# Projection and V moved to the end of TensorE's quarter, and the transposes of h made in tiles of 64 only

## The chip, the cores and the metric

The kernel runs on one core of one Trainium2 chip. Its engines are TensorE (PE; its weight loads are shown apart as PEld), VectorE (DVE), ScalarE (ACT), GpSimd (POOL) and SyncE (SP), which here issues all transfers. The metric is the device time of one execution in microseconds, the median of several runs.

## The reference, cut to what matters

A macaron block on x of shape 16 x 512 x 128, in float32: half a feed-forward part, attention with its residual, half a feed-forward part again.

```python
x = x + 0.5 * ffn(layernorm(x), w_gate, w_up, w_down)
x = x + attn(layernorm(x), w_q, w_k, w_v, w_proj, b_proj, ln_gamma, ln_beta)
x = x + 0.5 * ffn(layernorm(x), w_gate, w_up, w_down)

def ffn(x, w_gate, w_up, w_down):          # hidden size 352
    h = silu(fp4_linear(x, w_gate)) * fp4_linear(x, w_up)
    return fp4_linear(h, w_down)
def fp4_linear(x, w):                      # blocks of 16 along the contraction
    return fp4_quant_dequant(x) @ fp4_quant_dequant(w).T
def attn(x, ...):                          # 16 heads of 64, 512 x 512 scores each
    o = softmax(q @ k.T * 64 ** -0.5) @ v
    y = o @ w_proj + b_proj + x
    return layernorm(y) * ln_gamma + ln_beta
```

## The kernel before

There are 16 images. In each, attention goes over 8 pairs of heads p, and each pair over 4 quarters s, one for each key tile of 128. `i = 8 b + p` counts the pairs over all images, and t = 4 p + s the 32 quarters of an image. Each engine has its own program, which runs over the same quarters with a body written out by hand; `steps` unrolls two images ahead and the last ones, and loops over two images at a time between them. Engines meet only at semaphores, each engine works strictly in its own order, and so a place in the body is the schedule. (The profile shows a 32-bit float matmul as two records, "x4" for a pair; a pair is two halves of 64 output partitions that run side by side.)

PE's quarter begins with `scores` (L943: eight matmuls into pS for ACT's exponential). At s = 3 the broadcast of the reciprocals follows (L1049, into pM). Then come `for_maxima` (L955, into pX, one or two pairs ahead, for the row maxima that DVE takes at L779), `times_v` (L970, into pO), and one piece that depends on s:

- s = 0: Q of pair i + 2 (L927, into pM), read by ACT (QH, L738) and then by DVE (QL, L901).
- s = 1: the projection of pair i - 3 (`project`, L991, into pX), added up by DVE in Yacc (L898); then K of pair i + 2 (L927, into pM), read by ACT (KH, L741) and then by DVE (KL, L905).
- s = 2: the row sums (L980, into pM).
- s = 3: a quarter of V (L1085, into pM), read by ACT (VA, L750).

The feed-forward parts of the neighbouring images run in between: F is the first one and works for the image after, L the last one and works for an image before. `first_ffn` and `last_ffn` give them pieces at fixed t, behind everything else of PE's quarter. On PE, F has the transposes of x at t = 0 (L239), gates at 1 to 4 (L256), ups at 5 to 8 (L267), the transposes of h at 12 to 15 (`pe_h`, L284), the down projection at 16 (`pe_down`, L295) and a transpose at 20. L has ups at 0 to 2 and 31, `pe_h` at 6 to 9, `pe_down` at 10, the transposes of x at 26 and gates at 27 to 30. Each part has one PSUM tile, pF, which its pieces use in turn.

h has 352 columns, two chunks of 128 and one of 96. `pe_h` transposes each chunk in two column tiles, 64 wide but for the last one of the third chunk, which is 32 wide. ACT copies all three into hqT, `pe_down` contracts them with wdT, the transposed w_down, and takes 96 rows of the third chunk. wdT is made at the start from a tile that POOL fills with zeros before the weights are loaded into it.

What the projection waits for: ON of pair i - 3 (`s_norm`), all row maxima of pair i + 1 (`s_max`, DVE L779 of the same quarter, since both use pX), and the Yacc add before it (`s_yacc`). `for_maxima` at s = 2 waits for the Yacc add of this projection. V waits for KL, for VA before it, and for ON (`s_norm`, DVE L888 of the same quarter), all for pM. K waits for QL, the row sums for KL, and the next Q for VA.

DVE's quarter: the reciprocal (s = 0), the feed-forward steps that read PSUM (silu L331, h L337), ON (s = 3), the maxima, the Yacc add (s = 1), QL (s = 0) or KL (s = 1), and then the other feed-forward steps (block maxima L165, rounding L186 and L188, moments of the norms). ACT's: the feed-forward reads of PSUM (tanh L310, copies L305 and L315), the exponential L731, the copies of this quarter, and the other feed-forward steps (L181, L142). POOL adds up exponentials for the row sums (L640, L646) and does the scalings of the quantization (L175, L193).

Of the kernel before, what the change touches and what calls it, by code (L numbers as in the profile page):

```python
# [13 lines left out]
ALU = mybir.AluOpType  # L14
# [6 lines left out]
NP = B * PAIRS  # L21
FF = 352
# [4 lines left out]
FP = 384  # L27
FT = FP // 128
# [36 lines left out]
def there(n, count):  # L65

    return not isinstance(n, int) or 0 <= n < count


def wait(eng, sem, count):  # L70

    if not isinstance(count, int) or count > 0:
        eng.wait_ge(sem, count)


def half(n):

    return slice(64 * n, 64 * n + 64)
# [118 lines left out]
class Ffn:  # L197
# [73 lines left out]
    def pe_h(self, pe, c, k):  # L271

        if k % 2 == 0:
            pe.wait_ge(self.qh.s_quant, 2 * c + k // 2 + self.w0 + 1)
        if k == 0:
            pe.wait_ge(self.s_h, 4 * c + 4)
        else:
            pe.wait_ge(self.s_hT, 4 * c + k)
        row = self.row(k)
        for ch in range(FT):  # L280
            for n in range(2):
                f0 = ch * 128 + 64 * n
                w = min(64, FF - f0)
                ins = self.nc.tensor.matmul(self.pF[64 * n:64 * n + w, ch * 128:(ch + 1) * 128], row[:, f0:f0 + w],  # L284
                                            self.ident[:, :], start=True, stop=True)
        ins.then_inc(self.s_hT_ps, 1)

    def pe_down(self, pe, c):

        pe.wait_ge(self.s_hT, 4 * c + 4)  # L290
        for t in range(T):
            for ch in range(FT):
                rows = min(128, FF - ch * 128)
                for n in range(2):
                    ins = self.nc.tensor.matmul(self.pF[half(n), t * D:(t + 1) * D],  # L295
                                                self.hqT[0:rows, ch, t * 128 + 64 * n:t * 128 + 64 * n + 64],
                                                self.wdT[0:rows, ch, :], start=ch == 0, stop=ch == FT - 1)
        ins.then_inc(self.s_down, 1)


# [75 lines left out]
def make_program(nc, x_in, w_q, w_k, w_v, w_proj, b_proj, gamma_in, beta_in, w_gate, w_up, w_down, out):  # L376
# [35 lines left out]
    with ExitStack() as scope:  # L412
# [95 lines left out]
        with nc.Block() as block:  # L508
            @block.sync
            def _(sp):  # L510
# [3 lines left out]
                for k, w in enumerate((w_gate, w_up)):  # L514
                    sp.dma_start(wraw[:, k, 0:256].rearrange("p (t d) -> p t d", t=2),
                                 w[0:256, :].rearrange("(t p) d -> p t d", p=128)).then_inc(s_wraw, 16)
                    sp.dma_start(wraw[0:FF - 256, k, 256:384], w[256:FF, :]).then_inc(s_wraw, 16)
                sp.dma_start(wraw[:, 2, 0:FF], w_down).then_inc(s_wraw, 16)
                for k, w in enumerate((w_q, w_k, w_v)):
                    sp.dma_start(w_raw[:, k, :], w).then_inc(s_raw, 16)  # L520
                sp.dma_start(wp[:, :, :], w_proj.rearrange("(j p) d -> p j d", p=128)).then_inc(s_wp, 16)
# [234 lines left out]
            def _(dve):  # L756
# [9 lines left out]
                                    ident[0:4, 2 + hd:3 + hd].broadcast_to([4, 64]), ALU.add).then_inc(s_ones, 1)  # L766
                dve.wait_ge(s_ones, 3)
                v.memset(LROW[:, :], 1.0).then_inc(s_ones, 1)
                dve.wait_ge(s_wraw, 80)
                F.qh.maxima(nc, dve, 0, F.h[:, 0:NW], slice(0, NW // BLK))  # L770
                F.qh.round(nc, dve, 0, F.mag[:, 0:NW], F.h[:, 0:NW])

# [102 lines left out]
                def body(b, p, bpar):  # L875
                    i = PAIRS * b + p
                    par = p % 2
                    for s in range(KT):
                        t = 4 * p + s
                        if s == 0 and there(i - 2, NP):  # L880
                            dve.wait_ge(s_lc, 32 * (i - 1))
                            v.reciprocal(REC[par][:, :, :], LC[par][:, :, :]).then_inc(s_rec, 1)
                        first_ffn_psum(b, t, bpar)
                        last_ffn_psum(b, t, bpar)
                        if s == 3 and there(i - 2, NP):
                            dve.wait_ge(s_rb, i - 1)
                            wait(dve, s_proj, i - 2)
                            v.tensor_tensor(ON[:, :], OT[(p - 2) % 4][:, :], pM[:, :], ALU.mult).then_inc(s_norm, 1)  # L888
                        if s < 2:
                            maxima(i + 1, p + 1, s + 2)  # L890
                        else:
                            maxima(i + 2, p, s - 2)
                        if s == 1 and there(i - 3, NP):
                            bo, yp = (b, bpar) if p >= 3 else (b - 1, 1 - bpar)
                            dve.wait_ge(s_proj, i - 2)
                            dve.wait_ge(s_y0, bo + 1)
                            wait(dve, s_yacc, i - 3)
                            v.tensor_tensor(Yacc[yp][:, :], pX[:, 0, :], Yacc[yp][:, :], ALU.add).then_inc(s_yacc, 1)  # L898
                        if s == 0 and there(i + 2, NP):
                            dve.wait_ge(s_qhi, i + 3)  # L900
                            v.scalar_tensor_tensor(QL[(p + 2) % 4][:, :], pM[:, :], SCALE, QH[(p + 2) % 4][:, :].bitcast(F32),  # L901
                                                   ALU.mult, ALU.subtract).then_inc(s_qlo, 1)
                        if s == 1 and there(i + 2, NP):
                            dve.wait_ge(s_khi, i + 3)
                            v.scalar_tensor_tensor(KL[(p + 2) % 4][:, :], pM[:, :], 1.0, KH[(p + 2) % 4][:, :].bitcast(F32),  # L905
                                                   ALU.mult, ALU.subtract).then_inc(s_klo, 1)
                        first_ffn(b, t, bpar)
                        last_ffn(b, t, bpar)
                steps(dve, body)
# [2 lines left out]
            def _(pe):  # L912
# [125 lines left out]
                def body(b, p, bpar):  # L1038
# [3 lines left out]
                    for s in range(KT):  # L1042
# [15 lines left out]
                        if s == 0 and there(i + 2, NP):  # L1058
# [4 lines left out]
                                pe.wait_ge(s_wp, 16)  # L1063
                            wait(pe, s_va, i + 3 if not isinstance(i, int) else min(i + 3, ROUNDS) if i >= 0 else (0, 2)[i + 2])
                            per_head(0, p2, x).then_inc(s_q, 1)
                        if s == 1 and there(i - 3, NP):
                            project(i, p)
                        if s == 1 and there(i + 2, NP):
                            pe.wait_ge(s_qlo, i + 3)
                            per_head(1, p2, x).then_inc(s_k, 1)  # L1070
                        if s == 2 and there(i - 1, NP):
                            row_sums(i - 1, 1 - p % 2)
                        if s == 3:
                            for r in rounds_at(i):
                                kt, of, xb = round_place(i, p, bpar, r)
                                pe.wait_ge(s_klo, i + 3 if not isinstance(i, int) else min(i + 3, NP))
                                wait(pe, s_va, r)
                                if there(i - 2, NP):
                                    pe.wait_ge(s_norm, i - 1)
                                elif there(i - 1, NP):  # L1080
                                    pe.wait_ge(s_lrow, i)
                                if p == 5:
                                    pe.wait_ge(s_xf, b + 2)
                                for n in range(2):
                                    ins = pe_.matmul(pM[half(n), :], xf[xb][:, kt * 128 + 64 * n:kt * 128 + 64 * n + 64],  # L1085
                                                     w_raw[:, 2, of * S:of * S + S], start=True, stop=True)
                                ins.then_inc(s_v, 1)
                        first_ffn(b, 4 * p + s, bpar)
                        last_ffn(b, 4 * p + s, bpar)
                steps(pe, body)  # L1090


# [20 lines left out]
```

## Time and profile before

| | |
|---|---|
| Median of 3 runs | 2568.18 us (2564.86 to 2571.95) |
| The profiled execution | 2570.78 us, span 2569.0 us |
| Mean granted clock of PE | 0.963 of full speed |
| Busy, share of the span | PE 90%, PEld 47%, DVE 67%, ACT 47%, POOL 55% |

The span runs from the first to the last instruction. Busy shares are means over the whole of it: the first 150 us (granted clock 0.76) and the last 249 us (0.86) work at a lower clock and with less beside each other than the middle, where an image takes about 152 us. Idle time of an engine is put down to what ended it.

### The profile page before, as it was taken

The numbers are of one execution on the slowest core, as the hardware profiler recorded it, in microseconds if no ns is written. First come the engines' busy times: TensorE is split into PE (matmuls) and PEld (weight loads), VectorE is DVE, ScalarE is ACT, GpSimd is POOL, SyncE is SP. The second block draws the span as 40 slices with busy tenths as digits, with TensorE's granted clock in tenths as the row PEclk, the third lists the DMA queues.
The fourth block names the chain that finished last, engine by engine and source line by source line (L and its number), as shares of the span: only waits on it lengthen the run. The fifth ranks groups of instructions, "written<-read, shape, count | busy, mean of one in ns | idle before, by whom it ended". The sixth has DMA issues, their size and how long they took to land.

```text
span 2569.0 us, 45690 instructions
## 1 busy us (share of the span) xinstructions
PE 2312.5 (90%) x16292; PEld 1220.1 (47%) x16292; DVE 1721.6 (67%) x2830; ACT 1202.1 (47%) x1813; POOL 1412.9 (55%) x1323
## 2 busy tenths in 40 slices
PE   3799899999999999999989998999999999999984
PEld 1344444545454454545444454454545455454542
DVE  4465677767677776767667676776767677765643
ACT  1345454545545454544545444454454545444431
POOL 2255555656556565556556555565655656555551
PEclk7799999999999999999999999999999999999985
DMA  1000000000000000000000000000000000000000
GB/s 49 5 6 2 3 5 6 6 2 10 3 6 6 2 10 2 10 2 6 6 3 10 2 10 3 6 6 2 10 3 6 6 2 10 2 6 2 6 2 9
DMA packets 167394, 16.40 MB, mean 6 GB/s; under 512 B 148160, under 2 KB 166784, under 8 KB 167168
## 3 DMA queue, kind: packets, MB, share of 16 engines
q1 hardware_dynamic: 167168, 13.39, 4.5%
q8 instruction: 142, 2.33, 0.4%
q14 instruction: 84, 0.69, 0.1%
HBM read 7.03 MB, written 4.19 MB: 4 GB/s over the span
## 4 chain that ended last, share of the span: by engine, by line
PE 67%; DVE 20%; issue 6%; ACT 6%; POOL 1%; DVEq 0%; DMA 0%; SPq 0%; ACTq 0%; POOLq 0%
PE pS L943 16%; PE pO L970 12%; PE pM L927 8%; DVE nmax L779 7%; PE pX L991 5%; PE pM L1085 5%; PE pX L955 4%; PE pM L980 3%; PE FpF L284 2%; PE LpF L284 2%; PE FpF L295 2%; PE LpF L256 2%; PE LpF L267 1%; DVE QL L901 1%; PE FpF L256 1%
## 5 line engine op out<-in xcount | busy, mean ns | idle before, releaser
L646 POOL TENSOR_TENSOR ES<-ES,E 128x512 f32<-128x512 f32 x512 | 693.4, 1375 | 265.1 <-ACT E L731 263.5
L779 DVE TENSOR_REDUCE nmax<-pX 128x2 fp32r<-128x1024 f32 x512 | 622.1, 1215 | 161.2 <-PE pX L955 158.3
L731 ACT ACTIVATE E<-pS 128x1024 f32<-128x1024 f32 x512 | 523.2, 1022 | 420.4 <-PE pS L943 408.7
L970 PE MATMUL pO<-E,VA 128*64 128x512 f32 x2048 | 554.6, 620 | 0.0
L640 POOL TENSOR_TENSOR ES<-E 128x512 f32<-128x512 f32 x256 | 320.5, 1274 | 366.0 <-ACT E L731 366.0
L943 PE MATMUL pS<-QH,KH 64*128 64x512 f32 x1024 | 258.7, 501 | 19.6 <-issue 15.1
L927 PE MATMUL pM<-xf,w_raw 128*64 128x512 f32 x1024 | 268.1, 600 | 3.1 <-DVE QL L901 2.4
L741 ACT ACTIVATE KH<-pM 128x512 fp32r<-128x512 f32 x128 | 76.6, 598 | 358.2 <-PE pM L927 358.2
L955 PE MATMUL pX<-KH,QH 64*128 64x512 f32 x1024 | 233.2, 405 | 4.2 <-DVE nmax L779 2.7
L943 PEld LDWEIGHTS pS<-QH,KH 64*128 64x128 f32 x1024 | 96.8, 185 | 285.2 <-issue 253.8
L991 PE MATMUL pX<-wp,ON 128*64 128x128 f32 x2048 | 141.6, 280 | 98.9 <-DVE nmax L779 79.3
L991 PEld LDWEIGHTS pX<-wp,ON 128*64 128x64 f32 x2048 | 111.5, 138 | 208.8 <-DVE nmax L779 147.6
L943 PE MATMUL pS<-QL,KH 64*128 64x512 f32 x1024 | 205.2, 397 | 0.0
L943 PE MATMUL pS<-SH,onesr 64*128 64x512 f32 x1024 | 205.1, 396 | 0.0
L943 PE MATMUL pS<-QH,KL 64*128 64x512 f32 x1024 | 204.5, 395 | 0.0
L955 PEld LDWEIGHTS pX<-KH,QH 64*128 64x128 f32 x1024 | 180.8, 306 | 32.9 <-DVE nmax L779 9.2
L898 DVE TENSOR_TENSOR Yacc<-pX,Yacc 128x512 f32<-128x512 f32 x128 | 88.5, 691 | 159.6 <-PE pX L991 159.6
L901 DVE SCALAR_TENSOR_TENSOR QL<-pM,QH 128x512 fp32r<-128x512 f32 x128 | 88.5, 691 | 137.4 <-ACT QH L738 136.6
L1085 PE MATMUL pM<-w_raw,xf 128*64 128x512 f32 x512 | 142.6, 633 | 42.0 <-DVE ON L888 40.2
L750 ACT ACTIVATE VA<-pM 128x512 f32<-128x512 f32 x128 | 76.4, 597 | 204.7 <-PE pM L1085 204.7
L970 PEld LDWEIGHTS pO<-E,VA 128*64 128x64 f32 x2048 | 101.7, 135 | 127.8 <-issue 127.8
L905 DVE SCALAR_TENSOR_TENSOR KL<-pM,KH 128x512 fp32r<-128x512 f32 x128 | 88.5, 691 | 104.2 <-ACT KH L741 104.2
(141 smaller groups left out, 3402.0 us busy)
## 6 DMA issues: line engine op xcount, KB each, us to landing
RROW<-RC SPq DMA_DIRECT2D x512, 2.0 KB, 2.0
xin<-in_L_attn_x SPq DMA_DIRECT2D x16, 256.0 KB, 2.8
SH<-nmax SPq DMA_DIRECT2D x256, 2.0 KB, 2.0
LC<-LROW SPq DMA_DIRECT2D x256, 2.0 KB, 2.1
out<-X SPq DMA_DIRECT2D x16, 256.0 KB, 2.3
w_raw<-in_L_attn_w_q SPq DMA_DIRECT2D x1, 512.0 KB, 4.0
w_raw<-in_L_attn_w_k SPq DMA_DIRECT2D x1, 512.0 KB, 5.6
w_raw<-in_L_attn_w_v SPq DMA_DIRECT2D x1, 512.0 KB, 6.7
```

The source lines that it names most:

```text
L284: ins = self.nc.tensor.matmul(self.pF[64 * n:64 * n + w, ch * 128:(ch + 1) * 128], row[:, f0:f0 + w], self.ident[:, :], start=True, stop=True)
L640: ins = g.tensor_tensor(ES[par][:, hd, :], E[0][:, hd, :], E[1][:, hd, :], ALU.add)
L646: ins = g.tensor_tensor(ES[par][:, hd, :], ES[par][:, hd, :], E[s][:, hd, :], ALU.add)
L731: a.activation(E[s][:, :, :], pS[:, :, :], ACT.Exp).then_inc(s_exp, 1)
L779: v.tensor_reduce(nmax[px % 2][:, :, t:t + 1], pX[:, :, :], AX.X, ALU.max, negate=True).then_inc(s_max, 1)
L901: v.scalar_tensor_tensor(QL[(p + 2) % 4][:, :], pM[:, :], SCALE, QH[(p + 2) % 4][:, :].bitcast(F32), ALU.mult, ALU.subtract).then_inc(s_ql ...
L927: ins = pe_.matmul(pM[half(hd), :], w_raw[:, k, p * 128 + 64 * hd:p * 128 + 64 * hd + 64], x, start=True, stop=True)
L943: ins = pe_.matmul(pS[:, hd, :], lhs, qq[half(hd), :], start=n == 0, stop=n == 3)
L955: ins = pe_.matmul(pX[:, hd, :], QH[f][half(hd), :].rearrange("p (q t) -> p t q", t=KT)[:, t, :], KH[f][half(hd), :], start=True, stop=True)
L970: ins = pe_.matmul(pO[half(hd), :], VA[of][:, kt, j * 128 + 64 * hd:j * 128 + 64 * hd + 64], E[kt][:, hd, :], start=kt == 0, stop=kt == KT ...
L991: ins = pe_.matmul(pX[half(n), 0, t * 128:(t + 1) * 128], ON[:, t * 128 + 64 * n:t * 128 + 64 * n + 64], wp[:, po, :], start=True, stop=True)
L1085: ins = pe_.matmul(pM[half(n), :], xf[xb][:, kt * 128 + 64 * n:kt * 128 + 64 * n + 64], w_raw[:, 2, of * S:of * S + S], start=True, stop=True)
```

## The change

In PE's program the projection (s = 1) and V (s = 3) move behind the feed-forward pieces of the quarter, and the projection so also behind K. In DVE's program the Yacc add moves behind QL and KL. The waits of each moved step are the same ones and move with it.

The transposes of h all become tiles of 64 columns: the last tile of the third chunk takes columns 288 to 351, of which 288 to 319 have been taken by the tile before it. The third chunk so fills 128 rows of hqT, 32 of them twice, and `pe_down` contracts all 128. wdT has zeros at the rows of the second taking: w_down is loaded in two transfers, its last 32 columns 32 places further on, and the gap keeps POOL's zeros. The semaphore that DVE waits for counts one transfer more.

```diff
--- before.py
+++ after.py
@@ -279,9 +279,8 @@
         row = self.row(k)
         for ch in range(FT):
             for n in range(2):
-                f0 = ch * 128 + 64 * n
-                w = min(64, FF - f0)
-                ins = self.nc.tensor.matmul(self.pF[64 * n:64 * n + w, ch * 128:(ch + 1) * 128], row[:, f0:f0 + w],
+                f0 = min(ch * 128 + 64 * n, FF - 64)
+                ins = self.nc.tensor.matmul(self.pF[half(n), ch * 128:(ch + 1) * 128], row[:, f0:f0 + 64],
                                             self.ident[:, :], start=True, stop=True)
         ins.then_inc(self.s_hT_ps, 1)
 
@@ -290,11 +289,10 @@
         pe.wait_ge(self.s_hT, 4 * c + 4)
         for t in range(T):
             for ch in range(FT):
-                rows = min(128, FF - ch * 128)
                 for n in range(2):
                     ins = self.nc.tensor.matmul(self.pF[half(n), t * D:(t + 1) * D],
-                                                self.hqT[0:rows, ch, t * 128 + 64 * n:t * 128 + 64 * n + 64],
-                                                self.wdT[0:rows, ch, :], start=ch == 0, stop=ch == FT - 1)
+                                                self.hqT[:, ch, t * 128 + 64 * n:t * 128 + 64 * n + 64],
+                                                self.wdT[:, ch, :], start=ch == 0, stop=ch == FT - 1)
         ins.then_inc(self.s_down, 1)
 
 
@@ -515,7 +513,8 @@
                     sp.dma_start(wraw[:, k, 0:256].rearrange("p (t d) -> p t d", t=2),
                                  w[0:256, :].rearrange("(t p) d -> p t d", p=128)).then_inc(s_wraw, 16)
                     sp.dma_start(wraw[0:FF - 256, k, 256:384], w[256:FF, :]).then_inc(s_wraw, 16)
-                sp.dma_start(wraw[:, 2, 0:FF], w_down).then_inc(s_wraw, 16)
+                sp.dma_start(wraw[:, 2, 0:FF - 32], w_down[:, 0:FF - 32]).then_inc(s_wraw, 16)
+                sp.dma_start(wraw[:, 2, FF:FP], w_down[:, FF - 32:FF]).then_inc(s_wraw, 16)
                 for k, w in enumerate((w_q, w_k, w_v)):
                     sp.dma_start(w_raw[:, k, :], w).then_inc(s_raw, 16)
                 sp.dma_start(wp[:, :, :], w_proj.rearrange("(j p) d -> p j d", p=128)).then_inc(s_wp, 16)
@@ -766,7 +765,7 @@
                                     ident[0:4, 2 + hd:3 + hd].broadcast_to([4, 64]), ALU.add).then_inc(s_ones, 1)
                 dve.wait_ge(s_ones, 3)
                 v.memset(LROW[:, :], 1.0).then_inc(s_ones, 1)
-                dve.wait_ge(s_wraw, 80)
+                dve.wait_ge(s_wraw, 96)
                 F.qh.maxima(nc, dve, 0, F.h[:, 0:NW], slice(0, NW // BLK))
                 F.qh.round(nc, dve, 0, F.mag[:, 0:NW], F.h[:, 0:NW])
 
@@ -890,12 +889,6 @@
                             maxima(i + 1, p + 1, s + 2)
                         else:
                             maxima(i + 2, p, s - 2)
-                        if s == 1 and there(i - 3, NP):
-                            bo, yp = (b, bpar) if p >= 3 else (b - 1, 1 - bpar)
-                            dve.wait_ge(s_proj, i - 2)
-                            dve.wait_ge(s_y0, bo + 1)
-                            wait(dve, s_yacc, i - 3)
-                            v.tensor_tensor(Yacc[yp][:, :], pX[:, 0, :], Yacc[yp][:, :], ALU.add).then_inc(s_yacc, 1)
                         if s == 0 and there(i + 2, NP):
                             dve.wait_ge(s_qhi, i + 3)
                             v.scalar_tensor_tensor(QL[(p + 2) % 4][:, :], pM[:, :], SCALE, QH[(p + 2) % 4][:, :].bitcast(F32),
@@ -904,6 +897,12 @@
                             dve.wait_ge(s_khi, i + 3)
                             v.scalar_tensor_tensor(KL[(p + 2) % 4][:, :], pM[:, :], 1.0, KH[(p + 2) % 4][:, :].bitcast(F32),
                                                    ALU.mult, ALU.subtract).then_inc(s_klo, 1)
+                        if s == 1 and there(i - 3, NP):
+                            bo, yp = (b, bpar) if p >= 3 else (b - 1, 1 - bpar)
+                            dve.wait_ge(s_proj, i - 2)
+                            dve.wait_ge(s_y0, bo + 1)
+                            wait(dve, s_yacc, i - 3)
+                            v.tensor_tensor(Yacc[yp][:, :], pX[:, 0, :], Yacc[yp][:, :], ALU.add).then_inc(s_yacc, 1)
                         first_ffn(b, t, bpar)
                         last_ffn(b, t, bpar)
                 steps(dve, body)
@@ -1063,13 +1062,15 @@
                                 pe.wait_ge(s_wp, 16)
                             wait(pe, s_va, i + 3 if not isinstance(i, int) else min(i + 3, ROUNDS) if i >= 0 else (0, 2)[i + 2])
                             per_head(0, p2, x).then_inc(s_q, 1)
-                        if s == 1 and there(i - 3, NP):
-                            project(i, p)
                         if s == 1 and there(i + 2, NP):
                             pe.wait_ge(s_qlo, i + 3)
                             per_head(1, p2, x).then_inc(s_k, 1)
                         if s == 2 and there(i - 1, NP):
                             row_sums(i - 1, 1 - p % 2)
+                        first_ffn(b, 4 * p + s, bpar)
+                        last_ffn(b, 4 * p + s, bpar)
+                        if s == 1 and there(i - 3, NP):
+                            project(i, p)
                         if s == 3:
                             for r in rounds_at(i):
                                 kt, of, xb = round_place(i, p, bpar, r)
@@ -1085,8 +1086,6 @@
                                     ins = pe_.matmul(pM[half(n), :], xf[xb][:, kt * 128 + 64 * n:kt * 128 + 64 * n + 64],
                                                      w_raw[:, 2, of * S:of * S + S], start=True, stop=True)
                                 ins.then_inc(s_v, 1)
-                        first_ffn(b, 4 * p + s, bpar)
-                        last_ffn(b, 4 * p + s, bpar)
                 steps(pe, body)
```

## Rows read from the trace of the kernel before

**Rows 1.** The page: PE, DVE busy by engine, and the chain that ended last
```profile
PE 2312.5 (90%) x16292; PEld 1220.1 (47%) x16292; DVE 1721.6 (67%) x2830; ACT 1202.1 (47%) x1813; POOL 1412.9 (55%) x1323
...
PE 67%; DVE 20%; issue 6%; ACT 6%; POOL 1%; DVEq 0%; DMA 0%; SPq 0%; ACTq 0%; POOLq 0%
```

**Rows 2.** Windows, 310 us: busy of PE, PEld, DVE, ACT, POOL; granted clock; DMA
```profile
460.00:770.00 310.00, 288.79 (x2108) 154.43 (x2104) 219.39 (x365) 152.53 (x231) 178.85 (x169) 0.99 0.05 6
```

**Rows 3.** Groups by line and form, PE: busy, mean ns | idle before, releasers
```profile
L1085 PE MATMUL pM<-w_raw,xf 128*64 128x512 f32 x512 | 142.6, 633 | 42.0 <-DVE ON L888 40.2 <-ACT VA L750 0.8
L991 PE MATMUL pX<-wp,ON 128*64 128x128 f32 x2048 | 141.6, 280 | 98.9 <-DVE nmax L779 79.3 <-issue 18.8 <-DVE ON L888 0.8
...
L284 PE MATMUL LpF<-ident,Lh 128*64 128x128 f32 x640 | 58.0, 292 | 13.2 <-POOL Lh L193 10.7 <-ACT LhqT L315 2.5
...
L284 PE MATMUL LpF<-ident,Lh 128*32 128x128 f32 x128 | 27.8, 302 | 0.0
```

**Rows 4.** Timeline of PE, t = 17 to 25: start, length, what [idle before]
```profile
621.03 0.50 PE L943 MATMUL pS<-QH,KH 64*128 64x512 f32 x2
...
622.06 0.39 PE L955 MATMUL pX<-KH,QH 64*128 64x512 f32 x2
...
635.84 1.09 PE L991 MATMUL pX<-wp,ON 128*64 128x128 f32 x16 [0.93 <-DVE nmax L779]
...
652.02 1.09 PE L991 MATMUL pX<-wp,ON 128*64 128x128 f32 x16 [1.51 <-DVE nmax L779]
```

**Rows 5.** Timeline of all engines around the projection at t = 5
```profile
556.56 1.09 PE L991 MATMUL pX<-wp,ON 128*64 128x128 f32 x16 [1.75 <-DVE nmax L779]
...
557.48 1.03 PE L927 MATMUL pM<-xf,w_raw 128*64 128x512 f32 x4
557.70 0.69 DVE L898 TENSOR_TENSOR Yacc<-pX,Yacc 128x512 f32<-128x512 f32 x1 [1.20 <-PE pX L991]
...
558.34 0.76 PE L267 MATMUL FpF<-wguT,FxqT 128*64 128x352 f32 x4
...
559.03 0.50 PE L943 MATMUL pS<-QH,KH 64*128 64x512 f32 x2
...
559.19 0.69 DVE L905 SCALAR_TENSOR_TENSOR KL<-pM,KH 128x512 fp32r<-128x512 f32 x1 [0.80 <-ACT KH L741]
```

**Rows 6.** Timeline around V at t = 11
```profile
589.52 0.67 DVE L888 TENSOR_TENSOR ON<-OT,pM 128x512 f32<-128x512 f32 x1
...
590.34 1.08 PE L1085 MATMUL pM<-w_raw,xf 128*64 128x512 f32 x4 [2.10 <-DVE ON L888]
```

**Rows 7.** Timeline of PE: three transpose calls and what follows each
```profile
532.63 1.04 PE L239 MATMUL FpF<-ident,Fxn 128*64 128x128 f32 x16
533.50 0.76 PE L267 MATMUL LpF<-wguT,LxqT 128*64 128x352 f32 x4
...
594.47 1.16 PE L284 MATMUL FpF<-ident,Fh 128*64 128x128 f32 x12
595.55 0.50 PE L943 MATMUL pS<-QH,KH 64*128 64x512 f32 x2
...
631.50 1.04 PE L239 MATMUL FpF<-ident,Fxm 128*64 128x128 f32 x16
632.47 0.50 PE L943 MATMUL pS<-QH,KH 64*128 64x512 f32 x2
```

**Rows 8.** The down projection's line: duration ns min/median/max, start, forms
```profile
L295 PE MATMUL LpF<-wdT,LhqT x768: 270/272/474, 431.6 to 2565.1; 128*64 128x128 f32 x128, 96*64 96x128 f32 x64
```

**Rows 9.** Timeline of DVE: its first maximum of the weights
```profile
6.95 1.35 DVE L165 TENSOR_REDUCE Fqh_amax<-Fh 128x72 f32<-128x1152 f32 x1 [3.12 <-DMA Fh<-in_L_ffn_w_down]
```

**Rows 10.** The rounding's line on DVE: duration ns min/median/max, start, forms
```profile
L188 DVE SCALAR_TENSOR_TENSOR Lh<-Lmag,Lh x32: 891/893/1947, 402.9 to 2550.1; 128x704 f32<-128x704 f32 x32
```

**Rows 11.** The tile h of L, instructions on ACT: duration ns min/median/max, start, forms
```profile
L310 ACT ACTIVATE Lh<-LpF x64: 464/466/468, 361.5 to 2534.1; 128x352 f32<-128x352 f32 x64
...
L181 ACT ACTIVATE Lmag<-Lh x32: 782/784/792, 397.4 to 2547.1; 128x704 f32<-128x704 f32 x32
```

## The prediction

> **What bounds the kernel now.** I read the page's busy times first: PE has work in nine tenths of the span, and the next engine, DVE, in two thirds [rows 1]. The chain that ended last says the same: two thirds of it are PE's own matmuls, a fifth is DVE, 6% is "issue" [rows 1]. The window over two images in the middle agrees, 288.8 of 310 us on PE at a granted clock of 0.99 [rows 2]. So PE's order of work sets the time, and a microsecond is saved by taking work off PE or a wait from in front of it. Ahead of the 21 us that PE idles in that window I looked by line: only two groups own much of it. The projection (L991) waited 98.9 us over the run, 79.3 of it seen as the row maxima of DVE (L779), and V (L1085) waited 42.0 us, nearly all for ON [rows 3]. The timeline tells where. Call a quarter of an image t = 4p + s, so t runs from 0 to 31. In the image from 529 to 683 us the projection stands in t = 1, 5, 9, ... 29, and waited 0.39, 1.75, 0.32, 1.00, 0.32, 0.93, 1.51 and 0.31 us: 6.53 per image; [rows 4] has t = 21 and 25, [rows 5] t = 5, and those below 0.4 and t = 13 lie in the same stretch and view. The 0.3 is the floor, the length by which a maximum outlasts `times_v` when DVE is punctual; the rest is DVE coming late. V waited 0.20 at t = 7, 2.10 at t = 11, 0.17 at t = 19 and less than 0.1 elsewhere; t = 11 is in [rows 6].
>
> **Part 1, the projection goes behind K and the pieces.** Nothing is added; PE's eight matmul pairs only move. What they used to wait for runs on meanwhile. The cover is K, 0.86 us from start to start (557.48 to 558.34), and where there is a feed-forward piece another 0.6 us for a gate or up (558.34 to 559.03, less the 0.1 us change of tile shape ahead of the scores) or 0.65 for a transpose piece [rows 5]. Those pieces stand at t = 1 (two), 5, 9, 13 and 29; at 17, 21 and 25 there is K alone. So the wait of t = 1, 9, 13, 17 and 29 is covered whole. At t = 5, 1.75 - 0.86 - 0.58 = 0.31 stays; at t = 21, 0.93 - 0.86 = 0.07; at t = 25, 1.51 - 0.86 = 0.65.
>
> K itself needs QL of the quarter before. At t = 5 QL ended near 553.2 and K would start at 554.6: no new wait. The gates and ups of s = 1 need a silu or h that DVE makes ahead of that quarter's maximum, so they are ready 1.2 us before what the projection waited for.
>
> On DVE, Yacc now stands behind KL. It is what comes late next: `for_maxima` of s = 2 needs pX, so it waits for Yacc. Yacc starts 1.14 us after the projection's start and takes 0.69 [rows 5], and the projection lasts 0.92, so it ends 0.91 after the projection does. PE reaches `for_maxima` 0.1 (the change of shape) and 1.03 us of scores later [rows 4], so 0.2 us are to spare where KL is out of the way. KL ended 1.54 us after K's end (558.34 to 559.88) [rows 5]. Where no piece stands between K and the projection, that is 0.6 us after the projection's end, Yacc ends at 1.2 to 1.3, and PE waits some 0.15 us: t = 17 and 21. At t = 25 KL fits inside the wait that stays.
>
> One price on ACT: V's copy VA at t = 3 now comes after the gate, then a 0.78 us `magic` of L and a 0.47 us tanh stand before the exponential of t = 4 [rows 11]. I make QH 0.26 us later, and from QL on DVE is back to back up to the maximum of t = 5, so t = 5 keeps 0.57 instead of 0.31.
>
> What stays per image is 0.57 + 0.07 + 0.65 + 0.30 = 1.59, times 16 = 25 us. **Part 1 gives 98.9 - 25 = 74 us.** Bounds: all 98.9; and, if DVE's lateness simply comes out elsewhere, only the 0.3 us floors, 8 x 0.3 x 16 = 38.
>
> **Part 2, V behind the pieces.** The pieces at t = 7 and 27 cover 0.3 us per image. But t = 11 has no piece, and there is the 2.10. DVE is busy without a break from KL of t = 9 to ON of t = 11, with a rounding and the moments of `norm_y` in it; ON came at 589.52, V at 590.34 [rows 6]. PE gains 0.32 + 0.33 us at t = 9 (the wait and a transpose), while DVE's stretch starts just 0.3 earlier, so V waits 2.4. 42.0 - 16 x 2.44 = 3. **Part 2 gives 3 us**; between 0, and 10 if DVE keeps pace.
>
> **Part 3, transposes in tiles of 64.** A call writes three chunks of 128 columns. Before, the call at 594.47 took 1.08 us to the next matmul at 595.55, for 12 records [rows 7]. A like one in pairs of 64, 16 records, took 0.87 us where 64-wide work follows (532.63 to 533.50) and 0.97 ahead of scores (631.50 to 632.47) [rows 7]. So a pass of two records side by side is 0.87 / 8 = 0.109, and the change of shape 0.10. Six passes are 0.65, with the change 0.75: 0.33 less per call. Before, the group of 32-wide tiles alone held PE for 27.8 us in 128 records, 0.217 a record, against 58.0 / 640 = 0.091 for the others [rows 3]. There are 64 calls in F and 64 in L: **128 x 0.33 = 42 us.** The added columns cost nothing in time, since moving data stays 128 columns, and copies and rounding are as before. Bounds: 0, and 128 x (1.08 - 0.65) = 55.
> The Trainium skill ("TensorEngine Tiling (Array Packing)", Key Properties) says that changing the tiling mode drains the engine; by it alone I would only know that one of two changes per call goes away. The rows give its price. Against the change speaks "TensorE: Matmul & The Clock Gate", LDWEIGHTS: a weight load takes columns / 1.2 ns, so 64 columns instead of 32 cost an estimated 27 ns a load, 256 loads, 7 us if nothing hid them, which would make the time 2457.
>
> The down projection with 128 rows for 96: the line takes 270 ns at the least and 272 in the median with both forms in it [rows 8], so rows of the array cost no time. Nothing.
>
> **Part 4, the start.** w_down comes in two transfers. DVE's first maximum waited for it, 3.12 us [rows 9]. One more issue and one more landing stand on that path; I take 1 us, between nothing and that wait once more, nearer to the low end since the transfers run side by side. The attention's weights behind it are first used past 80 us.
>
> **Sum.** 74 + 3 + 42 - 1 = 118. The profiled execution took 2570.8 us (span 2569.0), so 2452.8; the runs' median is 2.6 lower: **2450**, 4.6% faster.
>
> **Rivals.**
> DVE becomes the bound in stretches. It has 219.4 of 310 us of work already [rows 2]; with the period down by 4.6% that is 74%, but uneven. And its two-input operations stretch while POOL works: the rounding takes 891 to 1947 ns [rows 10]. A shift of PE's order can put more of them on POOL's. Then PE waits again, at V or at `for_maxima`. With half of part 1 lost: 2450 + 37 = 2487. Against it: even in t = 5, where it was latest, DVE had time to wait, 1.20 us for the projection and 0.80 for KH [rows 5].
> The transposes keep their cost (the last pair still runs one after the other, as the 32-wide tile now does behind its neighbour): 2450 + 42 = 2492. Against it: [rows 7].
> DVE gains instead. KL a microsecond earlier lets its pieces start earlier, and the 2.4 at t = 11 and the 0.65 at t = 25 go: 16 x 2.2 = 35 less, 2415.
> Slower than before: `for_maxima` waits for Yacc in each of the 128 pairs. The gain is 118 / 128 = 0.92 us per pair, and Yacc has 0.2 to spare, so it must end 1.1 us later than worked out, in every pair. For it: Yacc is now the last link, K, KH, KL, Yacc. Against: KL lies under the projection but for 0.6 us. With 1.3 us it gives 2450 + 128 x 1.1 = 2591.
>
> **Chances.** Likeliest 0.68 (2428 to 2472), DVE bound 0.15, transposes unpaid 0.04, DVE gains 0.08, slower 0.03, no change 0.02 (within 0.3%, about what a measurement of this kernel can tell). Range: 2422 to 2489, which reaches into the first and third of the rivals. Faster 0.95, same 0.02, slower 0.03.
>
> **What would show it.** L991's idle before it down from 98.9 to about 25, found at t = 5 and 25; L1085's near 39, all of it at t = 11; no 128*32 form and L284 at 0.75 us per call; small new idle ahead of L955, some 5 us; the exponentials, and PE's busy time, otherwise as now. I am wrong if L955 or L1085 idle by tens of us more.

## The result and the profile after

| | before | after |
|---|---|---|
| Median | 2566.5 us (4 runs) | 2436.2 us (2435.2 to 2437.2, 4 runs) |
| The profiled execution's span | 2569.0 us | 2433.4 us |
| PE, DVE busy | 90%, 67% | 93%, 71% |

The changed kernel takes 0.9492 of the time before, with an interval of 0.9471 to 0.9514: some 130 us less. 2450 had been forecast, with a range of 2422 to 2489.

The page of the changed kernel, its engines and its chain that ended last, beside [rows 1]:

```profile
PE 2259.7 (93%) x16292; PEld 1212.9 (50%) x16292; DVE 1726.2 (71%) x2830; ACT 1195.0 (49%) x1813; POOL 1406.3 (58%) x1323
...
PE 74%; DVE 17%; issue 4%; ACT 4%; POOL 1%; DMA 0%; SPq 0%; DVEq 0%; ACTq 0%; POOLq 0%
```

PE's groups by line and form, beside [rows 3]. L990 is now the projection, L1086 is V, L283 is `pe_h`, L954 is `for_maxima`:

```profile
L954 PE MATMUL pX<-KH,QH 64*128 64x512 f32 x1024 | 251.3, 433 | 5.5 <-DVE nmax L778 2.6 <-ACT KH L740 1.4
...
L1086 PE MATMUL pM<-w_raw,xf 128*64 128x512 f32 x512 | 140.0, 625 | 38.5 <-DVE ON L887 37.8 <-ACT VA L749 0.8
L990 PE MATMUL pX<-wp,ON 128*64 128x128 f32 x2048 | 137.1, 276 | 20.3 <-DVE nmax L778 15.4 <-issue 4.1 <-DVE ON L887 0.8
...
L283 PE MATMUL LpF<-ident,Lh 128*64 128x128 f32 x768 | 58.6, 292 | 14.6 <-POOL Lh L193 11.5 <-ACT LhqT L313 3.1
L283 PE MATMUL FpF<-ident,Fh 128*64 128x128 f32 x768 | 55.7, 282 | 8.4 <-POOL Fh L193 6.5 <-ACT FhqT L313 1.9
```

The reader sees the idle ahead of the projection down from 98.9 to 20.3 us, that ahead of V nearly as before (42.0, now 38.5), and no 128*32 form. One number hides something: L954's busy time was 233.2 us with 405 ns a record, and is 251.3 with 433. Nobody gave it more work. A matmul whose weights come late is shown as a longer one, not as a wait.

The clearest view is the length of PE's quarters, from the start of one `scores` to the next in the timeline, as means in us over images 2 to 13 (the whole image from 152.2 to 143.6 us; quarters that are not listed moved by less than 0.03):

| quarter t | before | after | what changed there |
|---|---|---|---|
| 1, 17, 29 | 5.89, 4.64, 5.23 | 5.28, 4.10, 4.69 | waits of 0.39, 0.32, 0.31 covered |
| 5, 21, 25 | 6.67, 5.24, 5.84 | 5.22, 4.64, 4.98 | 1.75, 0.93, 1.51 became 0.30, 0.32, 0.66 |
| 9, 13 | 5.62, 6.31 | 4.76, 4.80 | wait covered, and a shorter `pe_h` |
| 2, 22, 26, 30 | 4.41, 3.22, 4.10, 3.82 | 4.60, 3.33, 4.21, 3.92 | longer, behind Yacc |
| 18 | 3.23 | 3.68 | longer, behind Yacc |
| 19 | 4.13 | 3.46 | `for_maxima` and V wait less for DVE, see below |
| 6, 14 | 4.80, 4.21 | 4.58, 3.98 | a shorter `pe_h`, less 0.1 behind Yacc |
| 10 | 5.87 | 5.95 | longer, behind Yacc |
| 7, 27 | 5.42, 4.35 | 4.70, 4.05 | V covered, at 7 a shorter `pe_h` |
| 8, 15 | 4.81, 4.43 | 4.48, 4.11 | a shorter `pe_h` |
| 11, 12 | 6.13, 4.52 | 6.39, 4.94 | V still waits, and the clock |
| 31, 0 | 5.33, 5.22 | 5.04, 4.96 | the end of a loop pass and the clock; medians 4.05, 4.70 and 4.05, 4.69 |

The timeline of the changed kernel from t = 17 to 18, beside [rows 4, 5], has two terms that the rows of idle time do not show:

```profile
589.25 1.03 PE L926 MATMUL pM<-xf,w_raw 128*64 128x512 f32 x4
...
590.11 1.04 PE L990 MATMUL pX<-wp,ON 128*64 128x128 f32 x16
...
590.96 0.69 DVE L898 SCALAR_TENSOR_TENSOR KL<-pM,KH 128x512 fp32r<-128x512 f32 x1 [1.27 <-ACT KH L740]
...
591.57 0.68 DVE L905 TENSOR_TENSOR Yacc<-pX,Yacc 128x512 f32<-128x512 f32 x1
...
592.32 0.34 PEld L954 LDWEIGHTS pX<-KH,QH 64*128 64x128 f32 x2 [0.47 <-issue]
592.35 0.62 PE L954 MATMUL pX<-KH,QH 64*128 64x512 f32 x2
...
592.90 0.20 PEld L969 LDWEIGHTS pO<-E,VA 128*64 128x64 f32 x4 [0.24 <-issue]
592.90 1.08 PE L969 MATMUL pO<-E,VA 128*64 128x512 f32 x4
```

First, a covered wait gave more than its idle time. At t = 17 before, `times_v` began at 617.75 and the projection at 619.14, 1.39 us; now `times_v` to K takes 0.91 (588.34 to 589.25). So the stall was 0.48 us, where its row says 0.32, since idle time is counted from the modelled end of the last matmul. Second, Yacc ends at 592.25, and the weight load of `for_maxima` starts at 592.32, where 591.89 + 0.23 would be its matmul's turn. Then `times_v` follows 0.55 us after that matmul; it was 0.33 (622.06 to 622.39) before. The quarter loses 0.45 us; only 0.07 of it is idle time of PE.

The next quarter gets that back, and a little more. The rows of t = 19, first before, then changed:

```profile
624.25 0.50 PE L943 MATMUL pS<-QH,KH 64*128 64x512 f32 x2
624.29 1.23 DVE L779 TENSOR_REDUCE nmax<-pX 128x2 fp32r<-128x1024 f32 x1
625.57 0.31 PEld L955 LDWEIGHTS pX<-KH,QH 64*128 64x128 f32 x2 [0.28 <-DVE nmax L779]
627.37 1.08 PE L1085 MATMUL pM<-w_raw,xf 128*64 128x512 f32 x4 [0.17 <-DVE ON L888]
```

```profile
594.08 1.23 DVE L778 TENSOR_REDUCE nmax<-pX 128x2 fp32r<-128x1024 f32 x1
594.76 0.51 PE L942 MATMUL pS<-QH,KH 64*128 64x512 f32 x2
597.28 1.03 PE L1086 MATMUL pM<-w_raw,xf 128*64 128x512 f32 x4
```

Before, the maximum of t = 18 ended at 625.52, and the weight load of the next `for_maxima` started right behind it; later V waited for ON. Now that maximum ends at 595.31, 0.55 us after the quarter's start instead of 1.27, and neither wait is left: V starts 2.52 us into the quarter instead of 3.12. Together t = 18 and 19 went from 7.35 to 7.14 us.

The clock by windows (span, busy PE, PEld, DVE, ACT, POOL, granted clock), two stretches of image 6, around V of t = 11 and from t = 11 to 12:

```profile
995.50:998.90 3.40, 3.24 (x10) 1.47 (x12) 1.26 (x3) 1.23 (x2) 2.74 (x4) 0.50 0.00 0
990.60:1002.10 11.50, 9.11 (x53) 4.45 (x51) 7.25 (x17) 4.50 (x6) 6.88 (x7) 0.85 0.04 3
```

```profile
995.66 1.98 PE L1086 MATMUL pM<-w_raw,xf 128*64 128x512 f32 x4 [2.39 <-DVE ON L887]
997.56 0.80 PE L942 MATMUL pS<-QH,KH 64*128 64x512 f32 x2
```

Just as V's wait of 2.4 us ends, the clock is granted at 0.50 for 3.4 us, and V takes 1.9 us to the next matmul instead of 1.0. Over images 2 to 14, which wait alike there, the clock fell between 0.6 us ahead of V's start and 1.6 us behind it in 6 of 13 before (wait 2.1 us) and in 10 of 13 now; it fell in image 1 too, where V waits 5.1 and 4.4 us.

### The profile page after: what moved, and what is told of

Same layout as the page of the kernel before. It is cut to its first block, busy times and chain, and to the rows that moved or that the text cites. A ratio compares the mean times of both kernels' runs of the same rounds, so it can differ in the third digit from the quotient of the medians.

```text
span 2433.4 us, 45691 instructions
## 1 busy us (share of the span) xinstructions
PE 2259.7 (93%) x16292; PEld 1212.9 (50%) x16292; DVE 1726.2 (71%) x2830; ACT 1195.0 (49%) x1813; POOL 1406.3 (58%) x1323
## 4 chain that ended last, share of the span: by engine, by line
PE 74%; DVE 17%; issue 4%; ACT 4%; POOL 1%; DMA 0%; SPq 0%; DVEq 0%; ACTq 0%; POOLq 0%
PE pS L942 19%; PE pO L969 17%; PE pM L926 8%; PE pX L954 5%; PE pX L990 5%; DVE nmax L778 4%; PE pM L1086 4%; PE pM L979 3%; PE LpF L283 2%; PE FpF L283 2%; PE FpF L293 2%; PE LpF L256 2%; PE LpF L267 2%; PE FpF L256 1%; PE FpF L267 1%
## 5 line engine op out<-in xcount | busy, mean ns | idle before, releaser
L645 POOL TENSOR_TENSOR ES<-ES,E 128x512 f32<-128x512 f32 x512 | 686.2, 1361 | 188.7 <-ACT E L730 188.4
L954 PE MATMUL pX<-KH,QH 64*128 64x512 f32 x1024 | 251.3, 433 | 5.5 <-DVE nmax L778 2.6
L954 PEld LDWEIGHTS pX<-KH,QH 64*128 64x128 f32 x1024 | 185.9, 306 | 46.2 <-issue 14.4
L1086 PE MATMUL pM<-w_raw,xf 128*64 128x512 f32 x512 | 140.0, 625 | 38.5 <-DVE ON L887 37.8
L898 DVE SCALAR_TENSOR_TENSOR KL<-pM,KH 128x512 fp32r<-128x512 f32 x128 | 88.4, 691 | 101.6 <-ACT KH L740 100.6
L990 PE MATMUL pX<-wp,ON 128*64 128x128 f32 x2048 | 137.1, 276 | 20.3 <-DVE nmax L778 15.4
L990 PEld LDWEIGHTS pX<-wp,ON 128*64 128x64 f32 x2048 | 115.9, 137 | 78.1 <-DVE nmax L778 47.9
L744 ACT ACTIVATE LROW<-pM 65x512 f32<-65x512 f32 x128 | 75.9, 593 | 154.4 <-PE pM L979 154.4
L926 PEld LDWEIGHTS pM<-xf,w_raw 128*64 128x64 f32 x1024 | 74.3, 140 | 153.9 <-issue 148.0
```

The lines of the kernel that those rows point to most:

```text
L645: ins = g.tensor_tensor(ES[par][:, hd, :], ES[par][:, hd, :], E[s][:, hd, :], ALU.add)
L926: ins = pe_.matmul(pM[half(hd), :], w_raw[:, k, p * 128 + 64 * hd:p * 128 + 64 * hd + 64], x, start=True, stop=True)
L954: ins = pe_.matmul(pX[:, hd, :], QH[f][half(hd), :].rearrange("p (q t) -> p t q", t=KT)[:, t, :], KH[f][half(hd), :], start=True, stop=True)
L990: ins = pe_.matmul(pX[half(n), 0, t * 128:(t + 1) * 128], ON[:, t * 128 + 64 * n:t * 128 + 64 * n + 64], wp[:, po, :], start=True, stop=True)
```

## The experiments

Each was compared with runs of the kernel before on the same chip; medians in us.

| run | median | ratio, interval |
|---|---|---|
| part 1 alone | 2490.8 | 0.9699 (0.9681 to 0.9717) |
| part 2 alone | 2571.8 | 1.0008 (0.9991 to 1.0025) |
| part 3 alone | 2558.1 | 0.9955 (0.9938 to 0.9973) |
| parts 1 and 3 | 2458.8 | 0.9557 (0.9536 to 0.9578) |
| changed, halves swapped | 2435.5 | 0.9470 (0.9447 to 0.9494) |
| changed, Yacc first | 2457.7 | 0.9552 (0.9531 to 0.9574) |
| changed, moments later | 2394.1 | 0.9320 (0.9303 to 0.9337) |
| the same, halves and Yacc | 2393.5 | 0.9305 (0.9285 to 0.9325) |
| before, filled | 2562.1 | 0.9977 (0.9963 to 0.9991) |
| part 3 alone, filled | 2529.8 | 0.9849 (0.9817 to 0.9881) |
| changed, filled | 2418.7 | 0.9417 (0.9387 to 0.9448) |

**Part 1 alone.** The kernel before with both moves of part 1:

```diff
-                        if s == 1 and there(i - 3, NP):
-                            project(i, p)
...
+                        if s != 3:
+                            first_ffn(b, 4 * p + s, bpar)
+                            last_ffn(b, 4 * p + s, bpar)
+                        if s == 1 and there(i - 3, NP):
+                            project(i, p)
                         if s == 3:
                             for r in rounds_at(i):
...
+                        if s == 3:
+                            first_ffn(b, 4 * p + s, bpar)
+                            last_ffn(b, 4 * p + s, bpar)
```

> The kernel before with the projection behind K and the pieces, and Yacc behind KL; V and the transposes as before. Theory A (a wait is worth the idle time that its row shows): L991's idle falls from 98.9 to some 20 us, 2568 - 79 = 2489, and t = 17 and 29, whose wait was 0.3, get shorter by 0.3 us each. Theory B (a wait costs its idle time and a refill of PE of about 0.2 us besides, and for_maxima of s = 2 gives 0.1 to 0.45 us back to Yacc): t = 17 and 29 shorten by 0.54, t = 18 grows by 0.45, and the sum is near 2568 - 81 = 2487. The sums are close, the quarters tell. Rival (DVE becomes the bound): 2510 or more, with V's idle up by tens of us.

79 us less. The projection's idle is 20.3 us, t = 17 and 29 are 0.54 us shorter (4.10, 4.69), t = 18 is 0.45 longer (3.68). The sum can't tell the theories apart; the quarters speak for B. Neither names t = 19, which is 0.66 us shorter here too, nor t = 12, which is 0.48 longer with the clock at half in it in 6 of images 2 to 13.

**Part 2 alone.** V behind the pieces:

```diff
+                        first_ffn(b, 4 * p + s, bpar)
+                        last_ffn(b, 4 * p + s, bpar)
                         if s == 3:
                             for r in rounds_at(i):
```

> The kernel before with V behind the pieces alone. Theory A: 0.3 us per image of covered idle, 5 us in all, 2563. Theory B: a refill of 0.2 us more at t = 7 and 27 each, 11 us, 2557. The prediction's price on ACT (QH 0.26 us late at t = 4 and with it the maximum of t = 5, which here is not covered) takes 4 us of either. V's idle stays near 35 us, all at t = 11.

No difference: both theories missed. t = 7 and 27 are shorter by 0.24 and 0.30 us, but t = 0, 11, 12, 15 and 31 are longer by 0.16 to 0.36 each. The clock can explain most of it: summed from the trace's clock records over images 2 to 13, half clock (the time in which 0.50 was granted) went from 34 us to 55 in the profiled executions. The price on ACT did not show, t = 5 stayed at 6.67.

**Part 3 alone.** `pe_h`, `pe_down` and the loads of w_down from the change, the order as before:

```diff
-                f0 = ch * 128 + 64 * n
-                w = min(64, FF - f0)
+                f0 = min(ch * 128 + 64 * n, FF - 64)
```

> The kernel before with the transposes of h in tiles of 64, the 128 rows of the third chunk and w_down in two transfers. If PE's time just adds: 128 calls x 0.33 us = 42, 2526. If DVE's stretches decide where they run from t = 9 to V at t = 11 and from Q at t = 12 to the maximum at t = 13: the calls at t = 9 and 12 turn into waits, 6 x 0.33 x 16 = 32, 2536, with the idle ahead of L991 up by 5 us and ahead of V by 5. Rival (the drain stays): 2568.

11 us less, where 42 or 32 were expected: both sums missed. The waits that the second theory names are there. The groups of that run:

```profile
L990 PE MATMUL pX<-wp,ON 128*64 128x128 f32 x2048 | 143.1, 282 | 104.0 <-DVE nmax L778 83.8 <-issue 19.4 <-DVE ON L887 0.8
...
L1084 PE MATMUL pM<-w_raw,xf 128*64 128x512 f32 x512 | 141.2, 627 | 51.0 <-DVE ON L887 49.3 <-ACT VA L749 0.8
```

The quarters t = 6, 8, 9, 14 and 15 are each 0.33 us shorter; t = 7 and 13 are not, since a wait took it (V at t = 7 now waits 0.53 us, the projection at t = 13 1.34), and V at t = 11 takes another 0.3. The rest fits the clock, which the filled kernels below try: half clock in images 2 to 13 is 72 us, against 34.

**Moments later.** The changed kernel with one step of DVE a quarter later, so that it stands behind ON:

```diff
-                        if t == 10:
+                        if t == 11:
                             dve.wait_ge(s_yacc, PAIRS * b)
                             norm_y.moments(nc, dve, c, Yacc[1 - bpar])
```

> The changed kernel with DVE's moments of norm_y a quarter later, at t = 11 behind ON and the maximum, in place of t = 10. They take 3.2 us of DVE ahead of ON, and V waits 2.4. If that stretch of DVE is all that holds V: its idle goes from 38.5 to under 5 us, 16 x (2.4 + 0.2) = 42 less, and the half clock that follows that wait in most images (3.4 us each time, some 1 us of time) goes too: about 2436 - 50 = 2386. Rival (DVE's lateness only moves on): ON is early, but the maxima at t = 12 and 13 come late, L954 or L990 idle 1 to 2 us more there, 2415 to 2436.

2394.1, 42 us less than the changed kernel; 2386 had been expected. Its groups and, at t = 13, its timeline:

```profile
L1086 PE MATMUL pM<-w_raw,xf 128*64 128x512 f32 x512 | 134.6, 604 | 4.7 <-DVE ON L887 3.9 <-ACT VA L749 0.8
```

```profile
564.78 1.09 PE L990 MATMUL pX<-wp,ON 128*64 128x128 f32 x16 [0.32 <-DVE nmax L778]
```

V's wait is gone. t = 11 went from 6.39 to 3.46 us and t = 12 from 4.94 to 3.90; t = 13 grew from 4.80 to 5.30, so a small part of DVE's lateness did move on, as the rival has it. t = 2 grew by 0.18. Half clock in images 2 to 13 fell from 44 us to 10.

**Parts 1 and 3, without V.** The changed kernel, with the pieces of s = 3 again behind V:

```diff
-                        first_ffn(b, 4 * p + s, bpar)
-                        last_ffn(b, 4 * p + s, bpar)
+                        if s != 3:
+                            first_ffn(b, 4 * p + s, bpar)
+                            last_ffn(b, 4 * p + s, bpar)
...
                                 ins.then_inc(s_v, 1)
+                            first_ffn(b, 4 * p + s, bpar)
+                            last_ffn(b, 4 * p + s, bpar)
```

> The changed kernel with V again ahead of the pieces, so parts 1 and 3 together. If V's move is worth nothing, as alone: 2436. If it covers what part 3 uncovers: with the transposes shorter V would wait 0.2 + 0.33 us at t = 7 and as before at t = 27, each with a refill of 0.2 us: some 1.0 us per image, 2452.

2458.8, more than the 2452 of the second theory: V's move, worth nothing alone, is worth 22 us in company. t = 7 is 5.35 against 4.70, t = 27 4.24 against 4.05, and t = 15, which had not been named, 4.53 against 4.11. Half clock is 58 us against 44, which is some 7 of the 22.

**Halves swapped.**

```diff
                         if t == 0:
                             pe.wait_ge(s_khi, x + 1)
-                            wait(pe, s_yacc, x - 4)
                         wait(pe, s_max, 4 * x + t)
                         f = px % 4
-                        for hd in range(2):
+                        for hd in (1, 0):
+                            if t == 0 and hd == 0:
+                                wait(pe, s_yacc, x - 4)
```

> The changed kernel, for_maxima of s = 2 with its two halves in the other order, and the wait for Yacc ahead of the second one only, which is the half of pX that Yacc reads. Theory B (the wait has to be over before the weight load, 0.23 us ahead of the matmul, and costs 0.1 to 0.45 us in each of eight quarters, 1.25 per image): some 0.9 of it comes back, t = 2, 10, 14, 22, 26 and 30 shorter by 0.1 each, 2422. Rival (PE stands in order anyway, or the halves no longer run side by side): 2436 or more.

Nearly the rival, and not the 2422 of theory B: t = 2, 10, 14, 22, 26 and 30 are shorter by 0.05 us, not 0.1, and the median stayed. Its timeline at t = 2:

```profile
515.11 0.69 DVE L905 TENSOR_TENSOR Yacc<-pX,Yacc 128x512 f32<-128x512 f32 x1 [0.82 <-PE pX L991]
...
515.70 0.46 PEld L955 LDWEIGHTS pX<-KH,QH 64*128 64x128 f32 x2
515.93 0.54 PE L955 MATMUL pX<-KH,QH 64*128 64x512 f32 x2
...
516.40 0.20 PEld L970 LDWEIGHTS pO<-E,VA 128*64 128x64 f32 x4 [0.24 <-issue]
```

Of the two loads merged in the row of 515.70, the second by itself:

```profile
515.86 0.31 PEld L955 LDWEIGHTS pX<-KH,QH 64*128 64x128 f32 x1
```

Both matmuls start on time, 0.23 us after the last one of the scores, but the second half's weights begin to load only when Yacc is done (515.80), and `times_v` comes 0.47 us after the matmuls instead of 0.33. So the load has to be early, not only the matmul; that the swap gives back half of the 0.1 us and no more is not explained further.

**Yacc first.** Yacc ahead of KL on DVE, all else changed:

```diff
-                        if s == 1 and there(i + 2, NP):
-                            dve.wait_ge(s_khi, i + 3)
-                            v.scalar_tensor_tensor(KL[(p + 2) % 4][:, :], pM[:, :], 1.0, KH[(p + 2) % 4][:, :].bitcast(F32),
-                                                   ALU.mult, ALU.subtract).then_inc(s_klo, 1)
                         if s == 1 and there(i - 3, NP):
...
+                        if s == 1 and there(i + 2, NP):
+                            dve.wait_ge(s_khi, i + 3)
+                            v.scalar_tensor_tensor(KL[(p + 2) % 4][:, :], pM[:, :], 1.0, KH[(p + 2) % 4][:, :].bitcast(F32),
+                                                   ALU.mult, ALU.subtract).then_inc(s_klo, 1)
```

> The changed kernel with Yacc again ahead of KL on DVE. If KL is what makes Yacc late in all quarters: 1.25 x 16 = 20 less, 2416. If KL holds Yacc up at t = 17 alone and Yacc otherwise is bound by the projection's end: 0.35 x 16 = 6 less at t = 18, but KL and all behind it come 0.6 us later at t = 9, so V waits 3.0 instead of 2.4 at t = 11, 10 more: 2441.

2457.7, 21 us more, where the second theory had 5. As it said, t = 18 is 0.35 us shorter and the other quarters of s = 2 aren't; V at t = 11 waits 2.97 us. Not foreseen: what t = 18 wins, t = 19 loses (0.53 us longer, V waits there again), t = 21 is 0.26 shorter, t = 2 is 0.23 longer, and half clock is 61 us. So the new order on DVE is part of the gain.

**Moments, halves and Yacc.** Moments later, halves swapped, and Yacc ahead of KL at p = 4 only:

```diff
+                        if s == 1 and p == 4 and there(i - 3, NP):
...
-                        if s == 1 and there(i - 3, NP):
+                        if s == 1 and p != 4 and there(i - 3, NP):
```

> The moments a quarter later (2394), with the halves swapped, and Yacc ahead of KL at t = 17 alone. If both small terms are as theory B has them: 14 and 3 us less, 2377. If the halves do nothing: 2391.

2393.5, the same as without them; 2377 or 2391 were expected. t = 18 and 21 win 0.41 and 0.26 us, t = 19 loses 0.59. So the wait for Yacc at t = 18 costs nothing that can be had back this way: with Yacc earlier, t = 18 and 19 together take 7.32 us, in the changed kernel 7.14.

**Filled.** Useless matmuls ahead of V at t = 11, in three kernels. They only add work, into a PSUM tile that is free there:

```diff
+                        if s == 3 and p == 2 and there(b + 1, B) and there(i - 2, NP):
+                            pe.wait_ge(F.s_h, 4 * b + 8)
+                            for k in range(2):
+                                for n in range(2):
+                                    pe_.matmul(F.pF[half(n), :], w_raw[:, 0, 64 * n:64 * n + 64], x, start=True, stop=True)
                         if s == 3:
                             for r in rounds_at(i):
```

> The changed kernel with two useless matmul pairs (1.7 us, into F's free PSUM tile) ahead of V at t = 11, inside its 2.4 us wait. If that wait is what lets PE's clock fall to half (44 us of half clock between images 2 and 13): half clock there falls to some 10 us and the time by about half of the rest, 2436 - 17 = 2419, with V's start unmoved. Rival (the clock has nothing to do with this wait): 2436, or a little more where the added pairs run into V.

> The transposes in tiles of 64 alone (2558, 72 us of half clock), with the same filling. If what part 3 earned went back through the clock: 2558 - 25 = 2533, and 20 to 26 us ahead of the kernel before with the filling. Rival (its gain is lost to waits alone): within 5 us of 2558.

> The kernel before with the same filling at t = 11, where V waits 2.1 us: 34 us of half clock between images 2 and 13, of which about half follows t = 11. 2568 - 9 = 2559. Rival: 2568 or more.

2418.7, 2529.8 and 2562.1, within 4 us of what the clock would give each (2419, 2533, 2559). The first two are far from their rivals; the last is 7 us below the kernel before, outside the interval but no more than the spread of its own runs (2559.9 to 2567.6). The changed kernel filled, by windows over t = 11 to 13 of image 6, and its timeline there:

```profile
984.70:996.20 11.50, 10.85 (x71) 5.58 (x71) 8.71 (x19) 5.21 (x8) 6.89 (x7) 1.00 0.03 2
```

```profile
987.21 1.89 PE L1078 MATMUL FpF<-xf,w_raw 128*64 128x512 f32 x8
...
989.74 1.08 PE L1091 MATMUL pM<-w_raw,xf 128*64 128x512 f32 x4 [0.65 <-DVE ON L887]
```

V starts 5.0 us after its quarter did, as without the filling (984.70 to 989.74; 990.61 to 995.66), but the clock stays at 1.00 and V is done a microsecond sooner. Half clock in images 2 to 13 is 7 us instead of 44; half of the difference is 19 us, and 17.5 were measured. In part 3 alone it is 14 instead of 72, in the kernel before 20.5 instead of 34. What is left in the changed and the part 3 kernel stands at the end of a loop pass. From before filled to part 3 filled, the tiles are worth 32 us, where 20 to 26 had been expected.

## Why the prediction was right

**What bounds the kernel** was read rightly: PE's order sets the time, and DVE at 76% of the middle stretch (234.3 of 310 us) did not take its place.

**Part 1, 74 us forecast, 79 measured alone.** The waits that were to stay were at t = 5, 21 and 25 and came out at 0.30, 0.32 and 0.66 us (forecast 0.57, 0.07, 0.65); 20.3 us of idle in all, 25 forecast. Three terms were mis-sized or missing, and two of them nearly cancelled, which is luck. A covered wait is worth some 0.2 us more than its idle time, 1.6 us per image. And the wait behind Yacc, forecast at 0.30 us per image, costs 1.25: there were 0.2 us to spare up to the matmul, as worked out, but the weight load starts 0.23 us earlier than the matmul, so all eight quarters of s = 2 lose some 0.1 us or more. Against the quarters before, s = 1 gained 6.31 us (without part 3) and s = 2 lost 1.25: 81 us in 16 images. The third term is t = 19, on which nothing had been forecast: 0.67 us per image, 11 us in all, of which 7 only return what t = 18 had lost. It hangs on the order on DVE: with Yacc first it falls to 0.13. It is a small form of the rival in which DVE gains, at another quarter than that rival names. The price on ACT at t = 5, 0.26 us, was not seen.

**Part 2, 3 us.** Its idle did what was said, down to 38.5 (39 forecast), with 2.38 us at t = 11 (2.44). But its worth isn't its idle: alone nothing, with the other parts 22 us, since the transposes' gain at t = 7 and 15 would have become a wait for ON. The prediction counted that gain as part 3's.

**Part 3, 42 us.** A call takes 0.65 us (550.75 to 551.40 in the changed kernel) or 0.75 ahead of scores, as worked out. Next to parts 1 and 2 the whole 0.33 came through at each call but that of t = 9, which went to V's wait at t = 11 as forecast. Alone they gave 11 us, filled 32. The trace agrees with the drain of the Trainium skill ("TensorEngine Tiling (Array Packing)", Key Properties) in that a change of shape costs 0.10 us [rows 7]; how the 0.33 us divide into the change of shape and the last pair that did not run side by side, no run shows. The 27 ns per load, estimated from the Trainium skill ("TensorE: Matmul & The Clock Gate", LDWEIGHTS), are about there: 110 to 112 ns a load for the 32-wide form and 142 to 147 for the other in the kernel before. They are hidden, since the calls came out at the length worked out without them.

**Part 4, a loss of 1 us.** No loss was seen: DVE's first maximum began at 6.50 us, and at 6.95 before.

**The sum**, 118, was 12 us short of the 130 measured, and that it came so near is in part luck. The quarters, times 16, give: part 1 with t = 19 92 us (74 forecast), the transposes 42, V's cover at t = 7 and 27 11, the longer wait and the clock at t = 11 and 12 a loss of 16 (part 2 had 3 for both together), and 9 at the end of the loop passes, t = 31 and 0: 138, against 136 between the two profiled executions. So part 1 came out 18 us better and part 2 8 us worse. The start is not it: half clock ahead of image 0 was 69 us before and 24 in the changed kernel, but image 0 begins at 101.6 us there and at 103.8 in "moments later" with 75 us of half clock, so some 2 us at most. The parts alone give 79, nothing and 11, so 40 us lie in how they work together; the clock and V's cover of the transposes account for most of it by the runs above, but one profile for each kernel doesn't divide it to 10 us. The end of a loop pass, where PE idles 2 to 4 us with nothing shown to wait for, differs by up to 2 us from one pass to the next in the same execution.

## What to carry to other kernels

Put behind a step's wait whatever is ready anyway, and ask of the moved step who waits for its reader: in this kernel the deadline of such a matmul was the start of its weight load, 0.23 us ahead of its own. Parts of a schedule change don't add, since one part's gain turns into a wait that another part covers; the worth of each alone can be nothing. And where one late step stays (V at t = 11 here), look upstream on the late engine: moving one step of DVE by a quarter gave another 42 us.

## What the runs showed of the hardware

In the changed kernel, whose PE is busy for 93% of the span, a wait of PE of 2.4 us at t = 11 was followed by 3.4 us or more at 1.2 GHz in 10 of the 13 images from 2 to 14; before, a wait of 2.1 us in 6. It cost the changed kernel 17.5 us, shown by taking it back with 1.9 us of useless matmuls in the wait. It also hid the worth of other changes: in part 3 alone the wait grew from 2.1 to 2.5 us and half clock from 34 to 72 us, and the same filling gave back 28 us. The Trainium skill ("TensorE: Matmul & The Clock Gate", "Why this matters for your kernels") warns of longer idle gaps between matmuls than these; here the shorter waits were enough.
